# First attention: V and the transposed probabilities as high and low fp32r parts, three products in place of one fp32 product

## The chip, the cores and the metric

The kernel runs on one core of a Trainium2 chip. The time is the device time of one execution in microseconds. An engine is called by its name in the profile: PE is TensorE (PEld its weight loads), DVE is VectorE, ACT is ScalarE, POOL is GpSimd, SP is SyncE, which here only issues DMAs.

## The reference, cut to what matters

Two layers, each attention-like block plus mixture of experts, on x of 2 x 1024 x 128 in fp32. The change touches the first attention, and of this batch 0 alone:

```
q = (xn @ Wq + bq) by 8 heads of 128;  k, v = xn @ Wkv + bkv, shared by the heads
q, k += sinusoidal positions
scores = q k^T / sqrt(128), causal
probs = softmax(scores);  attn = probs @ v;  out = attn (heads side by side) @ Wo
```

Behind it come a top-1 mixture of 14 experts (gelu), a selective scan (16 states, 256 channels, a recurrence over 1024 steps) and a top-2 mixture of 8 experts.

## The kernel before, in words

**Stages.** Layer norm, transposes and router logits of both batches; keys and values of batch 0; attention of batch 0 (`attention_first`, 8 heads, from about 38 to 234 us); keys and values of batch 1; the 32 tiles of the first experts, four at a time; attention of batch 1 beside the scan of batch 0; then the second experts beside the scan of batch 1. The order on each engine is written out by hand, one instruction queue per engine, tied by semaphores. DVE, ACT and PE each have their own `head` function with the same loop over `i` from 0 to 7.

**A head** (number g) works in eight iterations i, one for each block of 128 rows of queries. Row block i sees (i + 1) x 128 keys. In iteration i:

- PE (lines 1069 to 1108) makes the scores of row block i (`scores`, in batch 0 with `three`: high and low fp32r parts of Q and K, three products), adds the causal mask (bf16), in iterations 1 and 5 makes a half of a query (`query`), and then turns row block i - 2 with 128 x 128 transposes (`turn`). In iterations 0 and 1 it turns blocks 6 and 7 of the head before. Between these stand the products of turned probabilities and V (`out_part`, line 1043) and the projection (`project`).
- DVE (lines 1598 to 1616) takes the negated row maximum of block i from PSUM (`neg_max`, L1577, up to 1024 columns), in iterations 1 and 5 moves a half of the query (`q_evac`, L1568), in iterations 3 and 7 adds a projected half to X in four instructions (`add_out`, L1595). In head 0 the steps of the first router stand behind the maxima (`routing`), two of them (L1510, L1511) behind the last one.
- ACT (lines 692 to 717) copies the turned block i - 2 out of PSUM into `PT` (`keep_turned`, L682) and then takes the exponentials of block i (`exps`, L689, with the row sum), which frees the scores' bank; it also copies outputs (`out_evac`) and the query's high part (`query_high`, L668). POOL makes the query's low part (L538).

**Banks and waits.** The turned blocks go alternately to PSUM banks 4 and 5. Row blocks 0 to 3 are one part each (128 to 512 columns); blocks 4 to 7 are two, the first always 512 columns, the second 128, 256, 384 and 512. These twelve parts are counted by c from 0 to 11. Before PE writes part c, it waits until ACT has copied part c - 2 of the same bank (`s_ed`, line 1024). The products of columns 0 to 511 of the queries (group 0, four of them: 512, 384, 256, 128 columns) wait for part 3; those of the other half (group 1, eight: five of 512, then 384, 256, 128) wait for part 10 and, from their fifth on, for part 11. `out_part(g, b, 0, 0)` and `(…, 1)` stand in iterations 6 and 7, `(…, 2)` and `(…, 3)` in iteration 0 of the next head, group 1 in its iterations 2 to 5.

**Last head.** `head_end` does what is left: turn 6, two products, turn 7, the eight products of group 1, two projections with a DVE update after each. PE goes on with batch 1 only after the last update (`s_we`), and SP starts the third group of expert weights only then.

**Memory.** `ROOM` is one array that the stages share. KB is 256 elements of a partition. `PT` lies at 29 to 53 KB, `V` at 10 to 14 KB. The first two groups of expert weights and rows, loaded during the attention, lie at 53 to 73 KB and 74 to 82 KB, the fourth group's rows at 90 to 92 KB.

## Time and profile before

| | us |
|---|---|
| median of 3 runs | 770.08 (768.84 to 777.02) |
| profiled execution, its time | 773.8 |
| its span, first to last instruction | 772.0 |
| PE busy in the span | 677.2 (88%) |
| DVE busy | 536.7 (70%) |
| ACT busy | 410.4 (53%) |
| POOL busy | 235.4 (30%) |
| PE matmuls of probabilities and V (L1043), both attentions | 141.7 in 384 records |

PE matmuls are pipelined, so the durations of neighbours overlap: what a matmul costs in a stream is the distance from its start to the next one's, not its own duration. One fp32 matmul with a V block as weights shows as two records. In a timeline a row may stand for several equal instructions in a row (x4), with the time from the first one's start to the last one's end. In brackets stands the idle time of the engine before it, and what it waited for.

### The profile page before, as it was taken

To read this page: it belongs to the slowest core of one execution; us is meant where nothing else is said; L and a number is where in the kernel's file an instruction comes from. 1 tells how busy PE (TensorE), PEld (TensorE's weight loads), DVE (VectorE), ACT (ScalarE), POOL (GpSimd) and SP (SyncE) were. 2 spreads that over 40 slices of the span, in tenths; PEclk is the share of its full clock that TensorE was granted. 3 is DMA by queue.
4 is the path that set the end of the run, shared out by engine and by line. 5 is a ranking of instruction groups with operands and counts; after the bars stand their busy time and mean duration, and the time that the engine had idled before them with its cause. 6 is when DMAs were issued, how large, how long until landed. Compare 5 with 4: busy or idle time off the path is not lost. (4 is left out here: it accounts for less than half of the span.)

```text
span 772.0 us, 11210 instructions
## 1 busy us (share of the span) xinstructions
PE 677.2 (88%) x3446; PEld 470.6 (61%) x3446; DVE 536.7 (70%) x830; ACT 410.4 (53%) x824; POOL 235.4 (30%) x183
## 2 busy tenths in 40 slices
PE   3988999999998989888899999998577889889575
PEld 2856777777766975444465566565532788888223
DVE  6165444444422225219899999999899799999998
ACT  1145665565641547375876676665543767576220
POOL 0012211221200007000023323324014846688874
PEclk9999999999996899899999999999759999999698
DMA  8400000000055671002267777868683445454112
GB/s 300 145 4 11 11 5 7 14 10 8 11 165 177 187 244 48 8 7 98 73 164 170 178 186 194 185 171 219 177 208 75 132 137 172 138 178 127 31 42 81
DMA packets 59806, 86.79 MB, mean 112 GB/s; under 512 B 7505, under 2 KB 35922, under 8 KB 59762
## 3 DMA queue, kind: packets, MB, share of 16 engines
q1 hardware_dynamic: 41330, 57.89, 24.1%
q0 software_dynamic: 7680, 23.08, 14.0%
q10 hardware_dynamic: 10752, 5.24, 2.3%
q8 instruction: 26, 0.43, 0.2%
q14 instruction: 18, 0.15, 0.1%
HBM read 54.60 MB, written 14.81 MB: 90 GB/s over the span
## 5 line engine op out<-in xcount | busy, mean ns | idle before, releaser
L1577 DVE TENSOR_REDUCE nmax<-PS 128x1 f32<-128x128 f32 (+7 forms) x128 | 96.1, 751 | 108.7 <-PE PS L1015 108.4
L1043 PE MATMUL PS<-ROOM 128*128 128x512 f32 (+3 forms) x384 | 141.7, 489 | 0.7 <-ACT ROOM L682 0.7
L682 ACT COPY ROOM<-PS 128x512 f32<-128x512 f32 (+1 forms) x192 | 85.9, 483 | 91.5 <-PE PS L1027 90.6
L689 ACT ACTIVATE ROOM<-PS,nmax 128x128 f32<-128x128 f32 (+7 forms) x128 | 95.7, 748 | 47.5 <-DVE nmax L1577 45.2
L559 POOL DMA_DIRECT2D ROOM<-ROOM x32 | 28.5, 890 | 212.7 <-DVE ROOM L1661 212.7
L1027 PE MATMUL PS<-CST,ROOM 128*128 128x128 f32 x576 | 85.1, 275 | 7.9 <-ACT ROOM L682 7.9
L1027 PEld LDWEIGHTS PS<-CST,ROOM 128*128 128x128 f32 x576 | 63.8, 141 | 35.1 <-issue 24.4
L1043 PEld LDWEIGHTS PS<-ROOM 128*128 128x128 f32 x384 | 65.0, 191 | 29.8 <-issue 25.8
L1012 PE MATMUL PS<-LATER 128*128 128x512 f32 (+2 forms) x192 | 73.5, 492 | 6.5 <-ACT ROOM L689 3.9
L1653 DVE TENSOR_TENSOR_SCAN ROOM<-ROOM 128x1024 f32<-128x1024 f32 x32 | 72.8, 2275 | 0.8 <-ACT ROOM L725 0.2
L538 POOL TENSOR_TENSOR QL<-ROOM,QH 128x512 fp32r<-128x512 f32 x16 | 20.3, 1269 | 169.0 <-ACT QH L668 169.0
L524 POOL DMA_INDIRECT rows_in<-XN,slot x48 | 65.6, 1367 | 20.0 <-issue 12.4
L530 POOL DMA_INDIRECT GA<-rows_out,slot x32 | 33.8, 1055 | 89.0 <-DMA rows_out<-ROOM 79.6
L603 POOL TENSOR_TENSOR ROOM<-ROOM 128x1024 f32<-128x1024 f32 x24 | 56.3, 2367 | 11.6 <-DVE ROOM L1834 11.6
L1012 PEld LDWEIGHTS PS<-LATER 128*128 128x128 f32 x192 | 33.6, 191 | 36.2 <-issue 24.7
L1209 PE MATMUL PS<-ROOM,LATER 128*128 128x128 f32 x384 | 53.4, 286 | 1.9 <-ACT ROOM L798 1.7
L1209 PEld LDWEIGHTS PS<-ROOM,LATER 128*128 128x128 f32 x384 | 50.7, 201 | 5.8 <-ACT ROOM L798 2.3
L1223 PE MATMUL PS<-ROOM,LATER 128*128 x384 | 50.9, 285 | 0.3
L998 PE MATMUL PS<-KH,QH 128*128 128x512 f32 (+2 forms) x96 | 46.9, 488 | 4.7 <-POOL QL L538 2.8
L1223 PEld LDWEIGHTS PS<-ROOM,LATER 128*128 128x128 f32 x384 | 47.6, 199 | 2.3 <-issue 1.9
L870 ACT ACTIVATE ROOM<-ROOM,a_sc 128x1024 f32<-128x1024 f32 x32 | 36.4, 1143 | 19.8 <-DVE ROOM L1821 17.1
L1595 DVE SCALAR_TENSOR_TENSOR X<-PS,rinv,X 128x128 f32<-128x128 f32 x128 | 35.7, 341 | 14.6 <-PE PS L1065 14.6
(178 smaller groups left out, 1248.3 us busy)
## 6 DMA issues: line engine op xcount, KB each, us to landing
ROOM<-bc_rows SPq DMA_DIRECT2D x32, 512.0 KB, 4.1
ROOM<-ROOM POOLq DMA_DIRECT2D x32, 512.0 KB, 6.0
LATER<-in_w SPq DMA_DIRECT2D x48, 256.0 KB, 2.9
ROOM<-in_w SPq DMA_DIRECT2D x32, 321.0 KB, 4.0
rows_in<-zero SPq DMA_DIRECT2D x20, 256.0 KB, 3.2
LATER<-rows_in SPq DMA_DIRECT2D x24, 128.0 KB, 2.5
rows_out<-ROOM ACTq DMA_DIRECT2D x24, 128.0 KB, 2.0
ROOM<-rows_in SPq DMA_DIRECT2D x8, 256.0 KB, 4.3
```

Of the source, the lines that this page charges most:

```text
L524: nc.gpsimd.indirect_dma_start(out=xs[m > 0][:, :], out_offset=bass.IndirectOffsetOnAxis(ap=slot[m][:, k, u:u + 1], axis=0), in_=XN[:, t, ...
L603: nc.gpsimd.tensor_tensor(YA1[:, c, :], YA1[:, c, :], HC[:, c, :], ALU.add).then_inc(s_ya, 1)
L682: nc.scalar.copy(dst, src).then_inc(s_ed, 1)
L689: nc.scalar.activation(PR[:, s, 0:nk], sc[:, 0:nk], ACT.Exp, bias=nmax[:, i % 4:i % 4 + 1], accum_out=rsum[:, i:i + 1]).then_inc(s_ex, 1)
L998: mm(dst, a[0][ra], b_[0][rb], start=first, stop=False, skip_group_check=True)
L1012: mm(dst, Q1[:, i * P:(i + 1) * P], K1[:, lo:hi], start=True, stop=False, skip_group_check=True)
L1027: r = nc.tensor.transpose(PS[:, 4 + c % 2, (j - lo) * P:(j - lo + 1) * P], PR[:, i % 2, j * P:(j + 1) * P], ident)
L1043: r = mm(PS[:, 6, lo:BANK], V[:, j, :], PT[:, 4 * group + j, lo:BANK], start=j == 0, stop=True, skip_group_check=True)
L1209: r = mm(PS[:, 5 + i, c * P:(c + 1) * P], mw1[:, 2 * s + i, c * P:(c + 1) * P], MXT1[:, 2 * s + i, :], start=True, stop=True)
L1223: r = mm(PS[:, 7, i * P:(i + 1) * P], MH1[:, 4 * i + c, :], second_w[:, bass.ds(e, 1), c * P:(c + 1) * P].rearrange("p o m -> p (o m)"), s ...
L1577: nc.vector.tensor_reduce(nmax[:, i % 4:i % 4 + 1], sc[:, 0:(i + 1) * P], AX_X, ALU.max, negate=True).then_inc(s_nm, 1)
L1653: nc.vector.tensor_tensor_scan(HS0, DA[:, c, :], drive, 0.0, ALU.mult, ALU.add).then_inc(s_xsn, 1)
```

## The change

In batch 0, V is kept as VH and VL and the turned probabilities as PTH and PTL, all fp32r. ACT's copies write the high parts (VH, PTH; the type of the destination rounds them). DVE subtracts the high part from the value that still is in PSUM and writes the low part. Each product of probabilities and V becomes three: high x high, high x low, low x high (`three`, as in the scores). PE's waits for a turned part in batch 0, for its bank and for its product, go to the new semaphore `s_el`, which DVE raises after its subtraction. In DVE's loop `turned_low` stands last in each iteration, behind `add_out`. Batch 1 stays as it is.

```diff
@@ -134,10 +134,18 @@
 
         KB = 256
         HEAD_END, MOE_END, END = 53 * KB, 90 * KB, 133 * KB
+        with ExitStack() as first_split:
+            def split_tile(name, shape, dt=F32R):
+                return first_split.enter_context(nc.sbuf_tensor(name, shape, dt))
+
+            split_tile("under_PTH", [P, 29 * KB], F32)
+            PTH = split_tile("PTH", [P, 12, BANK])
+            split_tile("under_PTL", [P, MOE_END + 2 * KB - HEAD_END], F32)
+            PTL = split_tile("PTL", [P, 12, BANK])
+            VH, VL = (split_tile(n, [P, TB, D]) for n in ("VH", "VL"))
+            split_tile("under_KH", [P, END - MOE_END - 34 * KB], F32)
+            KH, KL, QH, QL = (split_tile(n, [P, T]) for n in ("KH", "KL", "QH", "QL"))
         ROOM = sb("ROOM", [P, END])
-
-        with ExitStack() as first_split:
-            KH, KL, QH, QL = (first_split.enter_context(nc.sbuf_tensor(n, [P, T], F32R)) for n in ("KH", "KL", "QH", "QL"))
         LATER = sb("LATER", [P, 4 * T])
         K1, Q1 = LATER[:, 0:T], LATER[:, T:2 * T]
 
@@ -233,6 +241,7 @@
         s_ke = sem("keys_ready")
         s_vp = sem("values_in_psum")
         s_ve = sem("values_ready")
+        s_vl = sem("values_low_ready")
         s_ein = sem("gate_exponent_in")
         s_eout = sem("gate_exponent_out")
         s_ohb = sem("onehot_ready")
@@ -254,6 +263,7 @@
         s_ex = sem("probs_ready")
         s_tc = sem("probs_transposed")
         s_ed = sem("probsT_ready")
+        s_el = sem("probsT_low_ready")
         s_pv = sem("head_out_in_psum")
         s_ue = sem("head_out_ready")
         s_ri = sem("inverse_sum_ready")
@@ -652,7 +662,7 @@
 
                 for q in (2 * b, 2 * b + 1):
                     act.wait_ge(s_vp, q + 1)
-                    nc.scalar.copy(V[:, 4 * (q % 2):4 * (q % 2) + 4, :], bank(VALUE_BANK[q])).then_inc(s_ve, 1)
+                    nc.scalar.copy((V if b else VH)[:, 4 * (q % 2):4 * (q % 2) + 4, :], bank(VALUE_BANK[q])).then_inc(s_ve, 1)
                     if b == 0:
                         act.wait_ge(s_kf, 2 * q + 2)
                         nc.scalar.copy(KH[:, (q % 2) * BANK:(q % 2 + 1) * BANK], QF).then_inc(s_kh, 1)
@@ -673,12 +683,12 @@
                 nc.scalar.activation(Q1[:, hf * BANK:(hf + 1) * BANK], bank(7), ACT.Identity, bias=bq[:, h:h + 1]
                                      ).then_inc(s_qr, 1)
 
-            def keep_turned(g, i):
+            def keep_turned(g, i, split=False):
 
                 for part in range(1 if i < 4 else 2):
                     c = i if i < 4 else 4 + 2 * (i - 4) + part
                     act.wait_ge(s_tc, 12 * g + c + 1)
-                    dst, src = turned(PT, i, part, c)
+                    dst, src = turned(PTH if split else PT, i, part, c)
                     nc.scalar.copy(dst, src).then_inc(s_ed, 1)
 
             def exps(g, i):
@@ -705,9 +715,9 @@
                     if i == 6 and pending:
                         out_evac(1, 2 * g)
                     if i < 2 and pending:
-                        keep_turned(g - 1, 6 + i)
+                        keep_turned(g - 1, 6 + i, split)
                     if i >= 2:
-                        keep_turned(g, i - 2)
+                        keep_turned(g, i - 2, split)
                     exps(g, i)
                     if i == 1 and not split:
                         query_out(g, 1)
@@ -730,9 +740,9 @@
                 with act.Fori(1, 7) as g:
                     head(g, True, True)
                 head(7, True, False, True)
-                keep_turned(7, 6)
+                keep_turned(7, 6, True)
                 out_evac(0, 15)
-                keep_turned(7, 7)
+                keep_turned(7, 7, True)
                 out_evac(1, 16)
 
             def front():
@@ -981,7 +991,7 @@
             logits(0)
             logits(1)
             pe.wait_ge(s_ke, 2)
-            pe.wait_ge(s_ve, 2)
+            pe.wait_ge(s_vl, 2)
 
             def query(g, h, b, hf):
 
@@ -1015,13 +1025,15 @@
                 mm(PS[:, s + i // 4, (i % 4) * P:(i % 4 + 1) * P], identb[:], causalb[:], start=False, stop=True,
                    skip_group_check=True).then_inc(s_qk, 1)
 
-            def turn(g, i, first=False):
+            def turn(g, b, i, first=False):
+
+                left = s_ed if b else s_el
 
                 pe.wait_ge(s_ex, 8 * g + i + 1)
                 for part in range(1 if i < 4 else 2):
                     c = i if i < 4 else 4 + 2 * (i - 4) + part
                     if not (first and c < 2):
-                        pe.wait_ge(s_ed, 12 * g + c - 1)
+                        pe.wait_ge(left, 12 * g + c - 1)
                     lo, hi = 4 * part, min(i + 1, 4 * part + 4)
                     for j in range(lo, hi):
                         r = nc.tensor.transpose(PS[:, 4 + c % 2, (j - lo) * P:(j - lo + 1) * P],
@@ -1030,18 +1042,23 @@
 
             def out_part(g, b, group, part, free=True):
 
+                ready = s_ed if b else s_el
                 if part == 0:
-                    pe.wait_ge(s_ed, 12 * g + (11 if group else 4))
+                    pe.wait_ge(ready, 12 * g + (11 if group else 4))
                     if group or not (isinstance(g, int) and g == 0):
                         pe.wait_ge(s_ue, 2 * g + group)
                     if not (group or free):
                         pe.wait_ge(s_rkr, b + 1)
                 if part == 2 and group:
-                    pe.wait_ge(s_ed, 12 * g + 12)
+                    pe.wait_ge(ready, 12 * g + 12)
                 for j in ((2 * part, 2 * part + 1) if group else (part,)):
                     lo = max(0, j - 4 * group) * P
-                    r = mm(PS[:, 6, lo:BANK], V[:, j, :], PT[:, 4 * group + j, lo:BANK], start=j == 0, stop=True,
-                           skip_group_check=True)
+                    if b:
+                        r = mm(PS[:, 6, lo:BANK], V[:, j, :], PT[:, 4 * group + j, lo:BANK], start=j == 0, stop=True,
+                               skip_group_check=True)
+                    else:
+                        r = three(PS[:, 6, lo:BANK], (VH, VL), (PTH, PTL), (slice(None), j, slice(None)),
+                                  (slice(None), 4 * group + j, slice(lo, BANK)), j == 0)
                 if part == 3:
                     r.then_inc(s_pv, 1)
 
@@ -1090,9 +1107,9 @@
                         parity[0] = 1 - s
                         query(g + 1, h + 1, b, 0)
                     if i < 2 and pending:
-                        turn(g - 1, 6 + i)
+                        turn(g - 1, b, 6 + i)
                     if i >= 2:
-                        turn(g, i - 2, isinstance(g, int) and g == 0)
+                        turn(g, b, i - 2, isinstance(g, int) and g == 0)
                     if i == 0 and pending:
                         out_part(g - 1, b, 0, 2)
                         out_part(g - 1, b, 0, 3)
@@ -1108,10 +1125,10 @@
                         out_part(g, b, 0, i - 6, not opening)
 
             def head_end(g, b, h):
-                turn(g, 6)
+                turn(g, b, 6)
                 out_part(g, b, 0, 2)
                 out_part(g, b, 0, 3)
-                turn(g, 7)
+                turn(g, b, 7)
                 for part in range(4):
                     out_part(g, b, 1, part)
                 pe.wait_ge(*((s_qr, 2 * g + 3) if g == HEADS else (s_we, 2 * g)))
@@ -1558,6 +1575,10 @@
                     ts(QF, QF, SCALE, None, ALU.mult).then_inc(s_kf, 1)
                     dve.wait_ge(s_kh, q + 1)
                     tt(KL[:, sl], QF, KH[:, sl].bitcast(F32), ALU.subtract).then_inc(s_ke, 1)
+                    dve.wait_ge(s_ve, q + 1)
+                    t4 = slice(4 * q, 4 * q + 4)
+                    tt(VL[:, t4, :], bank(VALUE_BANK[q]).rearrange("p (t d) -> p t d", d=D), VH[:, t4, :].bitcast(F32),
+                       ALU.subtract).then_inc(s_vl, 1)
 
             keys_values(0)
 
@@ -1576,6 +1597,14 @@
                 sc = PS[:, 2 * s:2 * s + 2, :].rearrange("p a n -> p (a n)")
                 nc.vector.tensor_reduce(nmax[:, i % 4:i % 4 + 1], sc[:, 0:(i + 1) * P], AX_X, ALU.max,
                                         negate=True).then_inc(s_nm, 1)
+
+            def turned_low(g, i):
+
+                for part in range(1 if i < 4 else 2):
+                    c = i if i < 4 else 4 + 2 * (i - 4) + part
+                    dve.wait_ge(s_ed, 12 * g + c + 1)
+                    dst, src = turned(PTL, i, part, c)
+                    tt(dst, src, turned(PTH, i, part, c)[0].bitcast(F32), ALU.subtract).then_inc(s_el, 1)
 
             def inverse(g, s, earlier=True):
                 dve.wait_ge(s_ex, 8 * g + 4 + 4 * s)
@@ -1612,6 +1641,10 @@
                         q_evac(g + 1, 0)
                     if i == 7 and pending:
                         add_out(g - 1, 1, x_prev)
+                    if i < 2 and pending and not batch[0]:
+                        turned_low(g - 1, 6 + i)
+                    if i >= 2 and not batch[0]:
+                        turned_low(g, i - 2)
                     for step in after.get(i, ()):
                         step()
 
@@ -1620,6 +1653,9 @@
                         6: lambda: tile_experts(m), 7: lambda: pick_weights(m)}
 
             def head_end(g):
+                if not batch[0]:
+                    turned_low(g, 6)
+                    turned_low(g, 7)
                 inverse(g, 1)
                 add_out(g, 0, True)
                 add_out(g, 1, True)
```

## Rows read from the trace of the kernel before

**Rows 1.** Stretch of heads 1 to 7: from:to, length, each engine's busy time, granted clock, DMA.

```profile
75.00:220.00 145.00, 144.31 (x797) 104.62 (x796) 61.20 (x123) 83.76 (x203) 28.82 (x26) 1.00 0.07 21
```

**Rows 2.** PE in order of time: start, us, what; heads 1, 6 and 7.

```profile
61.45 0.94 PE L1027 MATMUL PS<-CST,ROOM 128*128 128x128 f32 x7
...
67.17 0.28 PE L1027 MATMUL PS<-CST,ROOM 128*128 128x128 f32 x1
...
197.84 0.23 PE L1015 MATMUL PS<-causalb,identb 128*128 128x128 bf16 x1
...
199.57 0.94 PE L1027 MATMUL PS<-CST,ROOM 128*128 128x128 f32 x7
...
202.33 1.04 PE L1027 MATMUL PS<-CST,ROOM 128*128 128x128 f32 x8
...
203.81 0.28 PE L1027 MATMUL PS<-CST,ROOM 128*128 128x128 f32 x1
...
205.64 1.05 PE L1065 MATMUL PS<-ROOM 128*128 128x128 f32 x8
...
207.00 0.40 PE L1000 MATMUL PS<-KH,QL 128*128 128x512 f32 x1
207.23 0.23 PE L1015 MATMUL PS<-causalb,identb 128*128 128x128 bf16 x1
...
210.00 0.27 PE L999 MATMUL PS<-KL,QH 128*128 128x128 f32 x1
210.11 0.27 PE L1000 MATMUL PS<-KH,QL 128*128 128x128 f32 x1
...
212.95 0.28 PE L999 MATMUL PS<-KL,QH 128*128 128x256 f32 x1
213.07 0.28 PE L1000 MATMUL PS<-KH,QL 128*128 128x256 f32 x1
```

**Rows 3.** DVE in order of time: 512-column operations, keys' stage and first experts.

```profile
33.58 0.75 DVE L1552 SCALAR_TENSOR_TENSOR ROOM<-PS,bk,ROOM 128x512 f32<-128x512 f32 x1
34.36 0.43 DVE L1558 TENSOR_SCALAR ROOM<-ROOM 128x512 f32<-128x512 f32 x1
35.47 0.69 DVE L1560 TENSOR_TENSOR KL<-ROOM,KH 128x512 fp32r<-128x512 f32 x1 [0.68 <-ACT KH L658]
...
255.91 0.69 DVE L1710 TENSOR_TENSOR ROOM<-PS,ROOM 128x512 f32<-128x512 f32 x1 [1.87 <-PE PS L1169]
```

**Rows 4.** DVE in order of time, end of head 6 and of head 7.

```profile
198.11 1.22 DVE L1577 TENSOR_REDUCE nmax<-PS 128x1 f32<-128x1024 f32 x1 [3.04 <-PE PS L1015]
199.25 1.12 DVE L1595 SCALAR_TENSOR_TENSOR X<-PS,rinv,X 128x128 f32<-128x128 f32 x4
200.28 0.28 DVE L1577 TENSOR_REDUCE nmax<-PS 128x1 f32<-128x128 f32 x1
...
219.61 1.22 DVE L1577 TENSOR_REDUCE nmax<-PS 128x1 f32<-128x1024 f32 x1 [2.66 <-PE PS L1015]
```

**Rows 5.** ACT in order of time: copy of row block 7's first half, head 7.

```profile
202.97 0.59 ACT L682 COPY ROOM<-PS 128x512 f32<-128x512 f32 x1 [0.71 <-PE PS L1027]
```

**Rows 6.** Head 0: a stretch, and DVE in order of time at its end.

```profile
52.00:64.00 12.00, 9.97 (x57) 7.45 (x56) 11.32 (x25) 6.83 (x14) 1.27 (x1) 1.00 0.00 0
...
61.75 1.22 DVE L1577 TENSOR_REDUCE nmax<-PS 128x1 f32<-128x1024 f32 x1
...
63.58 0.29 DVE L1577 TENSOR_REDUCE nmax<-PS 128x1 f32<-128x128 f32 x1
```

**Rows 7.** PE in order of time: the eight last products of head 7.

```profile
223.99 5.86 PE L1043 MATMUL PS<-ROOM 128*128 128x512 f32 x16 [0.24 <-ACT ROOM L682]
```

**Rows 8.** PE in order of time: the router logits ahead of the first query.

```profile
30.91 6.85 PE L948 MATMUL PS<-wgate,XNT 128*128 128x14 f32 x32
```

**Rows 9.** A stretch, and PE in order of time, between head 7 and batch 1's keys.

```profile
230.00:235.00 5.00, 2.56 (x16) 2.02 (x15) 2.25 (x8) 0.47 (x1) 0.00 (x0) 0.93 0.00 0
...
234.33 3.66 PE L966 MATMUL PS<-XNT,ROOM 128*128 128x512 f32 x4 [1.22 <-DVE X L1595]
```

## The prediction

> **What bounds the kernel now.** I started from the stretches (the view that sums each engine's busy time). In 145 us of heads 1 to 7 of the first attention, PE is busy 144.31 us at full granted clock, DVE 61.20 and ACT 83.76 [rows 1]. The reader should see that nothing but PE's stream of work sets the pace there, and that DVE looks as if it had room. Then PE's timeline, for the period: the one-block transpose of row block 0 starts at 67.17 in head 1 and at 203.81 in head 7 [rows 2], so a head takes 136.64 / 6 = 22.77 us. Last the order of work on DVE and ACT around one head's end, because the change puts twelve instructions into DVE's queue and lets PE wait for them.
>
> **What it removes.** Twelve products of probabilities and V per head (six 512 wide, two each of 384, 256 and 128), each two records. One transpose (0.11) and four records of 512 go from 203.81 to 205.64, so a record is 0.43 and a 512-wide product 0.86 us; by columns 384 is 0.64, 256 is 0.43, 128 is 0.215. Sum 6 x 0.86 + 2 x (0.64 + 0.43 + 0.215) = 7.73 us.
>
> **What it adds on PE.** Three fp32r products each. The kernel has such products already, in the scores: start to start 0.23 at 512, 0.12 at 256, 0.11 at 128 [rows 2]; between these 384 is 0.18 (an estimate). Three times (6 x 0.23 + 2 x (0.18 + 0.12 + 0.11)) = 6.60 us. So PE is spared 1.13 us a head: 0.17 for each product of 512, 0.10 for 384, 0.07 for 256, and 0.12 lost for each of 128. By iteration of the head that is -0.34 in 2 and in 3, -0.27 in 4, +0.05 in 5, -0.17 in 6, -0.10 in 7, +0.05 in 0. The narrow rows show that three products do not cost three quarters of an fp32 one at every width. The Trainium skill (FP8 and Floating Point Precision, "TensorE Precision Notes") says that true fp32 makes four passes through the array, while reduced precision reads fp32 and truncates it. By that rule, with one pass per reduced product, the saving would be a quarter of 7.73, 1.93 us; the 128-wide row, as dear as the 256-wide, speaks against it.
>
> **What it adds on DVE.** Twelve subtractions per head, from PSUM and SBUF into fp32r. No row has exactly this. The nearest are 0.69 for 512 columns: from PSUM and SBUF into f32, and from SBUF alone into fp32r [rows 3]. Ends: 0.43, the multiply by a constant in SBUF, and 0.75, bias and position added from PSUM, both for 512 [rows 3]. I take 0.69, and by the maxima's 128 columns at 0.28 [rows 4] I put 0.42 at 256 and 0.55 at 384. The next DVE instruction starts about 0.08 before the one ahead ends: the 1.22 us maximum is followed after 1.14 [rows 4]. All twelve cost about 6.7 us, which DVE has. But it works in order, and PSUM bank and product now wait for the subtraction, not for ACT's copy. Two places have no room.
>
> **Stretch A, end of iteration 7 to the transposes of row block 6.** These need the bank whose first half of row block 5 must be subtracted. In DVE's queue that subtraction stands behind the 1024-column maximum of iteration 7 and four updates of X. Now: last score product 197.84, DVE's maximum 198.11, updates 199.25, done at 200.28 [rows 2, 4]. The subtraction then takes 0.69, and an engine starts some 0.06 after the one it waits for (200.28 + 0.69 + 0.06 = 201.03). PE started these transposes at 199.57. From 197.84 that is 3.19 instead of 1.73: **+1.46**; the 0.10 spared in iteration 7 is inside it, lost.
>
> **Stretch B, from there to the transposes of row block 0.** They need the first half of row block 7. PE reaches that turn 2.76 us later (199.57 to 202.33), plus 0.05 for the narrow products. ACT begins its copy 0.64 later (202.97) and takes 0.59 [rows 5]; then 0.05, 0.69, 0.06. Sum 4.84 instead of 4.24 (199.57 to 203.81): **+0.60**.
>
> **Rest of the head.** Iterations 2 to 6 keep their lead (a maximum, a copy and a subtraction fit between the turns of one bank), and PE gains 0.34 + 0.34 + 0.27 - 0.05 + 0.17 = 1.07. A head thus takes 1.46 + 0.60 - 1.07 = **0.99 us longer**. From head 1 to head 7: six times, 5.9 us.
>
> **Head 0.** Routing shares DVE, busy 11.32 of 12 us [rows 6]. Subtractions of row blocks 1 to 4 (less 0.08 each: 0.34 less what little idle there is, 0.27; 0.48; 0.61; 0.61 and 0.20) come ahead of the last maximum, which moves from 61.75 to about 63.9. From this maximum to the next, 61.75 to 63.58, are 1.83 us; then 0.69 and 0.06: the transposes of block 6 start at 66.5 instead of 61.45, and with B's 4.84 those of head 1's block 0 at 71.4 instead of 67.17 [rows 2]: +4.2. The cover that hid ACT's copies in head 0 is gone.
>
> **Tail.** In head 7 iterations 2 to 6 give back 1.07. From the last maximum (219.61) the group of eight products began 4.38 later, at 223.99 [rows 4, 7]. Now there are 1.14 + 1.03 + 0.69 + 0.06 = 2.92 to the turn of block 6, then twice copy and subtraction with nothing between, 2 x 2.03: 6.98, +2.6. The eight products are 5 x 0.17 + 0.10 + 0.07 - 0.12 = 0.9 shorter. Tail +1.7.
>
> **Costs nothing.** The low parts of V, two times 0.69 on DVE, fall under the 6.85 us of router logits that start at 30.91 and end at 37.8 [rows 8]: the key's last subtraction starts at 35.47, 0.6 later with one before it, and the last of V ends at 37.5. If the logits were shorter, 1.4 us would show. ACT writes its copy in another type, same size. The new tiles lie in the room of later stages; the first two groups of expert weights do not touch them. All that follows waits for attention's end, so the delay is passed on whole.
>
> **Clock.** PE stood half idle from 230 to 235, and its next four records of 512 took 3.66 us instead of 1.72 [rows 9]: half speed, 1.2 GHz for a few us. In head 0 PE now waits three times for DVE, each time behind a routing step: for block 3's subtraction (the second part of block 4's turn needs its bank), for block 4's near 63.8, just ahead of the last maximum, and for block 5's until 66.5. So I add one such loss, 1.9 us, in head 1. The Trainium skill (TensorE: Matmul & The Clock Gate, "What's actually happening") has the half rate as the default that activity lifts; these rows agree.
>
> **Sum.** 4.2 + 5.9 - 1.07 + 1.7 + 1.9 = 12.6 us on the profiled execution's 773.8. That stands 0.5% above the median 770.08, which I scale from: **782.7**.
>
> **Rivals.**
> 1. *PE stays the bound, both waits covered.* Then only PE's sum counts: 8 x 1.13 = 9.0 us less, **761.1**, faster. For it: DVE is under half busy. Against: stretch A has 1.6 us of PE work over a chain of 3.2; it decides only if the maximum, the updates and the subtraction together fall under half of what the rows say. 0.06.
> 2. *Each fp32r product costs a quarter of the fp32 one at every width*, as it nearly does at 512 (0.23 of 0.86). Then a head is spared a quarter of 7.73, 1.93 instead of 1.13: 0.80 more, 6.4 in all, **776.3**, within 1%. Against it the 128-wide rows. 0.09. (The page of the Trainium skill on floating point, named above, would have it so.)
> 3. *The subtraction costs 0.43.* A and B fall by 0.26 each, a head is +0.47, head 0 +2.9, tail +0.9: 5.5 us without a clock loss, **775.6**. 0.09.
> 4. *The waits of 1.6 and 0.6 us let the clock fall in every head.* Six more times 1.9: **794**. For it: the wait before 234.33 was only 1.22. Against: from 52 to 64 PE is idle for 2 of 12 us and keeps full clock [rows 6]. 0.09.
>
> The forecast keeps 0.67. With 0.75 for a subtraction and the clock lost twice it gives 787; with small errors in the handovers 789. Range 775.5 to 789: it takes in rivals 2 and 3. Within 1% (762.4 to 777.8) is what a measurement can't tell from no change: rivals 2 and 3 less some, plus a little of the forecast's own spread, 0.17. Slower 0.77, faster 0.06.
>
> **What would show it.** PE waits for DVE's subtraction ahead of block 6's turn, about 1.5 us, and of block 0's, about 0.5, in each head; head period 23.8; the subtraction 0.69 at 512; head 1's block 0 turned near 71; DVE near 16 us of each head. It is wrong if the period is below 22.8, if PE has no idle time named for DVE, or if later stages take in the delay.

## The result and the profile after

The changed kernel took 783.38 us in the median of 20 runs (776.23 to 791.28), against 771.08 us of 20 runs of the kernel before. The ratio of the compared runs is 1.0139, with a 95% interval of 1.0106 to 1.0171: slower by 1.1 to 1.7%, or some 8 to 13 us. The ratio leaves out the three runs that stand more than 1.5% above the fastest of their kernel (788.31 and 791.28 after, 777.02 before). The prediction was 782.7.

One profiled execution is worse evidence than these medians, since the clock's phases differ from run to run. The one of after took 777.78 us with a span of 775.9, only 3.9 more than before. Cut in three: up to the first query it was 2.5 us quicker (first query at 35.09, before 37.60). The **stage** from that query to the first key product of batch 1 took 243.26 - 35.09 = 208.17 us, before 234.33 - 37.60 = 196.73: +11.4. What follows was 5.0 us shorter (775.9 - 243.26 against 772.0 - 234.33), where the change has nothing to do and the clock was kinder: granted clock 0.94 in the first 56 us of that part instead of 0.85 (that this accounts for all 5.0 us is not shown). So I compare stages below; whole times stand beside them with their ratios.

The stretch of heads 1 to 7, as in [rows 1] (columns as there):

```profile
75.00:220.00 145.00, 133.46 (x825) 110.07 (x824) 93.73 (x195) 82.04 (x196) 28.90 (x26) 1.00 0.03 9
```

PE's busy time fell from 144.31 to 133.46 us at full clock, and DVE's rose from 61.20 to 93.73. Neither is full now: the stretch has 11.5 us in which PE waits. The view of waits for 75 to 215 us (who waited for whom: us in total, times, longest) says for whom; before, PE had no wait in it:

```profile
DVE nmax L1598 <- PE PS L1025: 38.8, 29, 2.3
PE PS L1039 <- DVE PTL L1607: 11.0, 12, 1.5
```

L1607 is the subtraction, L1039 the transposes (L1027 before). Twelve waits in six heads, two each. PE in order of time in head 1, at the end of head 6 and in head 7, to be held against [rows 2], and the last group, against [rows 7]:

```profile
68.47 0.30 PE L1039 MATMUL PS<-CST,ROOM 128*128 128x128 f32 x1 [0.46 <-DVE PTL L1607]
...
187.94 0.30 PE L1039 MATMUL PS<-CST,ROOM 128*128 128x128 f32 x1 [0.45 <-DVE PTL L1607]
...
203.70 0.23 PE L1025 MATMUL PS<-causalb,identb 128*128 128x128 bf16 x1
...
206.97 0.95 PE L1039 MATMUL PS<-CST,ROOM 128*128 128x128 f32 x7 [1.50 <-DVE PTL L1607]
...
211.89 0.30 PE L1039 MATMUL PS<-CST,ROOM 128*128 128x128 f32 x1 [0.45 <-DVE PTL L1607]
...
233.81 0.50 PE L1008 MATMUL PS<-PTH,VH 128*128 128x512 f32 x1 [0.96 <-DVE PTL L1607]
```

The head period is (211.89 - 68.47) / 6 = 23.90 us, before 22.77. DVE at the same place, to be held against [rows 4]:

```profile
203.97 1.22 DVE L1598 TENSOR_REDUCE nmax<-PS 128x1 f32<-128x1024 f32 x1 [1.99 <-PE PS L1025]
205.11 1.12 DVE L1624 SCALAR_TENSOR_TENSOR X<-PS,rinv,X 128x128 f32<-128x128 f32 x4
206.15 1.01 DVE L1607 TENSOR_TENSOR PTL<-PS,PTH 128x512 fp32r<-128x512 f32 x2
```

The reader should see the chain: DVE waited 1.99 us for the last scores, then maximum, four updates and two subtractions run without a gap, and PE, idle for 1.50 us, starts at 206.97, about 0.13 after the first subtraction's end (206.15 + 0.69). A single subtraction of 512 columns took what the nearest rows had ([rows 3]; this one is in head 7):

```profile
221.71 0.69 DVE L1607 TENSOR_TENSOR PTL<-PS,PTH 128x512 fp32r<-128x512 f32 x1
```

### The profile page after: what moved, and what is told of

It reads as the page before. It is cut to its first block and busy times, and to the rows that moved or that the text cites. A ratio compares the mean times of both kernels' runs of the same rounds, so it can differ in the third digit from the quotient of the medians.

```text
span 775.9 us, 11548 instructions
## 1 busy us (share of the span) xinstructions
PE 658.3 (85%) x3530; PEld 476.0 (61%) x3542; DVE 582.5 (75%) x928; ACT 412.3 (53%) x824; POOL 235.2 (30%) x183
## 5 line engine op out<-in xcount | busy, mean ns | idle before, releaser
L1039 PE MATMUL PS<-CST,ROOM 128*128 128x128 f32 x576 | 86.0, 276 | 25.1 <-DVE PTL L1607 18.5
L1039 PEld LDWEIGHTS PS<-CST,ROOM 128*128 128x128 f32 x576 | 63.9, 141 | 53.8 <-issue 25.3
L692 ACT CAST PTH<-PS 128x512 fp32r<-128x512 f32 (+2 forms) x96 | 43.2, 483 | 75.2 <-PE PS L1039 75.2
L1057 PE MATMUL PS<-ROOM 128*128 128x512 f32 (+1 forms) x192 | 70.9, 490 | 0.5 <-ACT ROOM L692 0.5
L1607 DVE TENSOR_TENSOR PTL<-PS,PTH 128x512 fp32r<-128x512 f32 (+2 forms) x96 | 50.3, 551 | 10.1 <-ACT PTH L692 9.4
L692 ACT COPY ROOM<-PS 128x512 f32<-128x512 f32 (+2 forms) x96 | 43.0, 485 | 25.9 <-PE PS L1039 25.1
L1226 PEld LDWEIGHTS PS<-ROOM,LATER 128*128 128x128 f32 x384 | 49.8, 198 | 5.8 <-ACT ROOM L808 2.4
L1240 PEld LDWEIGHTS PS<-ROOM,LATER 128*128 128x128 f32 x384 | 46.2, 194 | 2.4 <-issue 2.1
L1624 DVE SCALAR_TENSOR_TENSOR X<-PS,rinv,X 128x128 f32<-128x128 f32 x128 | 35.8, 342 | 11.4 <-PE PS L1082 11.4
```

The lines of the kernel that those rows point to most:

```text
L692: nc.scalar.copy(dst, src).then_inc(s_ed, 1)
L1039: r = nc.tensor.transpose(PS[:, 4 + c % 2, (j - lo) * P:(j - lo + 1) * P], PR[:, i % 2, j * P:(j + 1) * P], ident)
L1057: r = mm(PS[:, 6, lo:BANK], V[:, j, :], PT[:, 4 * group + j, lo:BANK], start=j == 0, stop=True, skip_group_check=True)
L1226: r = mm(PS[:, 5 + i, c * P:(c + 1) * P], mw1[:, 2 * s + i, c * P:(c + 1) * P], MXT1[:, 2 * s + i, :], start=True, stop=True)
L1240: r = mm(PS[:, 7, i * P:(i + 1) * P], MH1[:, 4 * i + c, :], second_w[:, bass.ds(e, 1), c * P:(c + 1) * P].rearrange("p o m -> p (o m)"), s ...
L1607: tt(dst, src, turned(PTH, i, part, c)[0].bitcast(F32), ALU.subtract).then_inc(s_el, 1)
```

## The experiments

The theory: the three products spare PE 1.13 us a head, and two waits for DVE's subtractions (stretch A before row block 6's turn, stretch B before block 0's) cost more. The rivals: the products are not cheaper; DVE's total load sets the pace; the clock. For each kernel stand the stage, the head period (from the one-block turn, the transpose of row block 0, of head 1 to that of head 7, divided by six), and the time from the first query to head 1's one-block turn ("head 0"). All three are read from one trace of each kernel. How far such a figure scatters can be seen in head 0: after and order have the same code there and stand 0.68 us apart, since PE came to full speed about 1 us later in order, counted from the first query; so differences under 0.7 us in head 0 say nothing. The period repeats to 0.03 where no edit touches it (after 23.90, head0 23.91, dup3 23.93).

| kernel | head 0 | period | stage | ratio to before, 95% interval |
|---|---|---|---|---|
| before | 29.57 | 22.77 | 196.73 | |
| after | 33.38 | 23.90 | 208.17 | 1.0139 (1.0106 to 1.0171) |
| p_only | 29.42 | 21.60 | 187.53 | 0.9833 (0.9765 to 0.9901) |
| w_only | 32.68 | 24.99 | 216.17 | 1.0224 (1.0158 to 1.029) |
| dup6 | 34.53 | 25.09 | 217.95 | one run |
| dup3 | 34.44 | 23.93 | 209.44 | one run |
| order | 34.06 | 22.91 | 201.83 | one run |
| cover | 33.63 | 22.65 | 202.23 | one run |
| head0 | 31.82 | 23.91 | 206.71 | one run |
| all3 | 31.38 | 21.73 | 191.10 | 0.9939 (0.9913 to 0.9965) |
| all5 | 32.88 | 21.75 | 191.30 | 0.9922 (0.9899 to 0.9945) |
| before_tail | 29.40 | 22.77 | 195.66 | 0.9999 (0.9979 to 1.0019) |
| all6 | 28.94 | 21.77 | 187.53 | 0.9843 (0.9804 to 0.9883) |

### p_only: the products alone

```diff
-                        r = three(PS[:, 6, lo:BANK], (VH, VL), (PTH, PTL), ...
+                        r = three(PS[:, 6, lo:BANK], (VH, VL), (PTH, PTH), ...
-                left = s_ed if b else s_el
+                left = s_ed
```

and no `turned_low` on DVE; `ready` likewise. The kernel leaves out the low part of the probabilities, so its result is not the attention's; PE's work is that of the changed kernel.

> Left out of the computation: the low part of the probabilities. The third product takes the high part again, DVE makes no such low part, and PE waits for ACT's copy as in the kernel before. PE's work is that of the changed kernel. Theory (PE is spared 1.13 us a head, the waits for DVE eat it): the head period falls from 22.77 to 21.64 us, PE has no waits in heads 2 to 7, and the stage from the first query to batch 1's keys takes 196.73 - 9.0 = 187.7 us; whole kernel about 9 us faster than before. Rival (the three products themselves cost more than rows of the scores say, by switching between fp32 and fp32r): period 22.8 or more, no gain.

Period 21.60 (expected 21.64), stage 187.53 (187.7), 9.2 under before. The stretch of 75 to 210 us:

```profile
75.00:210.00 135.00, 134.39 (x855) 112.12 (x855) 60.31 (x122) 83.60 (x203) 28.78 (x26) 1.00 0.06 18
```

PE is the bound again, with less work per head. The saving is shown, and the products' rival is out.

### w_only: the waits alone

```diff
-                    dst, src = turned(PTH if split else PT, i, part, c)
+                    dst, src = turned(PT, i, part, c)
-                    if b:
+                    if True:
                         r = mm(PS[:, 6, lo:BANK], V[:, j, :], PT[:, 4 * group + j, lo:BANK], ...
-                    tt(dst, src, turned(PTH, i, part, c)[0].bitcast(F32), ...
+                    tt(dst, src, turned(PT, i, part, c)[0], ...
```

(and V instead of VH, for the copy and the subtraction of V, likewise).

> PE's products stay single fp32 ones from the fp32 copies; DVE makes the low parts all the same (nobody reads them) and PE waits for DVE's subtraction instead of ACT's copy. Theory: stretch A takes 3.27 instead of 1.73 us and stretch B 4.87 instead of 4.24, so the head period is 22.77 + 1.54 + 0.63 = 24.94 us; head 0 as in the changed kernel +3.8, tail +2.8: the stage takes about 196.73 + 3.8 + 13.0 + 2.8 = 216.3 us, whole kernel about 19 to 20 us slower than before. Rival (the longer stage comes from the new products, DVE's load is covered): period 22.8, no change.

Period 24.99 (expected 24.94), stage 216.17 (216.3). PE in head 7:

```profile
215.37 0.95 PE L1039 MATMUL PS<-CST,ROOM 128*128 128x128 f32 x7 [1.38 <-DVE PTL L1607]
...
220.25 0.30 PE L1039 MATMUL PS<-CST,ROOM 128*128 128x128 f32 x1 [0.46 <-DVE PTL L1607]
```

The two waits stand at the same places without the new products. Alone they cost 2.22 us a head (24.99 - 22.77); with the products they cost 23.90 - 21.60 = 2.30.

### dup6 and dup3: the same instruction at two places of the queue

```diff
+            spare = room(126 * KB, [4, P])
...
+                    if c == 6:
+                        tt(spare, src, turned(PTH, i, part, c)[0].bitcast(F32), ALU.subtract)
                     tt(dst, src, ...).then_inc(s_el, 1)
```

(`c == 3` in dup3).

> The changed kernel, with the subtraction of row block 5's first half (512 columns) done twice, the first time into a spare place. Theory (this one stands in the chain from the maximum of iteration 7 to PE's turn of block 6): all of its 0.61 us shows in each head; period 23.90 + 0.61 = 24.5 us, stage 208.2 + 8 x 0.61 = 213.0 us. Rival (DVE's total load sets the pace, or a fixed overhead of waiting): also +0.61; told apart by dup3.

> The changed kernel, with the subtraction of row block 3 (512 columns) done twice, the first time into a spare place. The same instruction as in dup6, at another place of the queue. Theory: in iteration 5 DVE has 0.7 us of idle time behind it, so the period stays within 0.1 us of 23.90; only head 0, where routing fills DVE, may grow by up to 0.6. Rival (DVE's total load sets the pace): +0.6 us per head, as in dup6.

dup3: period 23.93, nothing of 0.61 us on a head, so DVE's total load is not the pace. Head 0 grew by 1.06, more than the 0.6 expected: the wait for block 3's subtraction by 0.56 (4.07 instead of 3.51), and behind it PE still ran at half speed when it turned block 5 (six transposes in 1.36 us, in the changed kernel 0.82). dup6: four of its six head periods are 24.41 to 24.64, which is the 0.61 expected; two are 26.15 and 26.24, which was not, and the stage is 217.95 where 213.0 was expected. In these two the clock fell; the second one (the granted clock is the third number from the end):

```profile
215.00:217.00 2.00, 0.89 (x8) 0.92 (x9) 1.57 (x5) 0.23 (x1) 0.00 (x0) 1.00 0.00 0
217.00:219.00 2.00, 2.00 (x12) 1.91 (x11) 1.21 (x3) 1.65 (x5) 0.00 (x0) 0.55 0.04 8
```

PE had waited 2.01 and 2.10 us just before. In the other four heads it waited 2.00 to 2.09 us and kept full speed, and so it did behind the waits of 1.40 to 1.50 us in heads 1 to 6 of the changed kernel. So the fourth rival of the prediction names something real, at 1.7 us per fall, but in heads 1 to 7 it did not strike the changed kernel, and the length of the wait alone does not say when it does (more of this in the last section).

### order, cover: two ways out of the waits

order, on DVE:

```diff
-                    if i == 7 and pending:
+                    if i == 7 and pending and batch[0]:
                         add_out(g - 1, 1, x_prev)
...
                     if i >= 2 and not batch[0]:
                         turned_low(g, i - 2)
+                    if i == 7 and pending and not batch[0]:
+                        add_out(g - 1, 1, x_prev)
```

> The changed kernel, with DVE's subtractions in iteration 7 put ahead of the four updates of X. Theory: the 1.03 us of the updates leave the chain of stretch A, whose wait of 1.50 us falls to 0.5; the updates' result is needed only by the query of the next iteration, 2 us later. Period 23.90 - 1.0 = 22.9 us, stage 208.2 - 7 x 1.0 = 201.2 us. Rival (PE waits then for the updates at the query, or for ACT's copy): the period falls by less than 0.5.

cover, on PE in batch 0:

```diff
+                    if i == 0 and pending and not b:
+                        out_part(g - 1, b, 0, 2)
+                        out_part(g - 1, b, 0, 3)
+                    if i == 2 and pending and not b:
+                        pe.wait_ge(s_qr, 2 * g + 2)
+                        project(g - 1, h - 1, 0)
                     if i < 2 and pending:
                         turn(g - 1, b, 6 + i)
```

(and these steps left out at their old places).

> The changed kernel, DVE untouched; on PE, in batch 0, the last two products of columns 0 to 511 go ahead of the turn of row block 6, and the first projection ahead of the turn of row block 0. Theory: work that waits for nothing fills the waits: 0.7 of stretch A's 1.50, all 0.45 of stretch B's; period 23.90 - 1.15 = 22.75 us. Rival (moving work ahead only moves the wait to the next step, since block 6's copy and subtraction start no earlier): period falls by less than 0.5.

order: period 22.91, expected 22.9. cover: 22.65, expected 22.75. The four updates are 1.0 of stretch A, and both waits are waits of order, not of throughput: in order both are still there, at 0.36 to 0.46 us, in cover B's is gone and A's is 0.7 to 0.8. cover's stage, 202.23, holds a tail partly at half speed (granted clock 0.50 from 225 to 230 us), which order's, 201.83, has not.

### head0, all3, all5: where head 0 did not follow

```diff
                     neg_max(g, i)
+                    early = beside and not batch[0] and i >= 2
+                    if early:
+                        turned_low(g, i - 2)
                     if beside and i in beside:
                         beside[i]()
...
-                    if i >= 2 and not batch[0]:
+                    if i >= 2 and not batch[0] and not early:
                         turned_low(g, i - 2)
...
+                steps = routing(0)
+                late_steps = {2: (steps.pop(6),), 4: (steps.pop(7),)}
```

> The changed kernel; in head 0 the subtractions go ahead of the routing steps of their iteration, and the last two routing steps move to iterations 2 and 4 of head 1. Theory: PE's waits of 3.51 and 1.17 us in head 0 come from subtractions that stood behind routing steps; both are under 0.5 then, and head 1's one-block turn comes 4 us earlier against the first query; the period of later heads stays 23.90. Stage about 204.5 us. Rival (DVE is full in head 0, order changes nothing): under 1 us.

> All three reorderings in one kernel. Theory: the waits of stretch A (1.50, less 1.0 and 0.7) and B are gone, the period is PE's own work, 21.7 us, head 0 costs nothing against the kernel before; the tail still pays copy and subtraction twice, about +1.8. Stage 196.73 - 7 x 1.07 + 1.8 - 1 = about 190 us, so 6 to 7 us faster than before, 17 faster than the changed kernel. Rival (ACT's copy or the maxima become the bound): period 22.3 or more and no gain over before.

head0 gained 1.6 of the 4 us expected. The wait of 3.51 for block 3 was 0.58, but one of 2.51 for block 4 came up, and behind it the clock fell. In all3 the three edits add up in the heads (period 21.73, PE's own work) and the kernel is faster than before, ratio 0.9939. Its stage is 191.10, expected 190.

I read the 2.51 as a matter of order again: ACT's copy of block 4 stood behind its cast of the query, and this behind `q_evac`, which DVE did after `row_slots`. all5 moved `q_evac` ahead of `row_slots` in head 0, and changed the tail of `head_end` in batch 0 (on DVE first, then on PE):

```diff
+                    if early and i == 5:
+                        q_evac(g + 1, 0)
                     if beside and i in beside:
                         beside[i]()
...
+                out_part(g, b, 0, 2)
+                out_part(g, b, 0, 3)
                 turn(g, b, 6)
-                out_part(g, b, 0, 2)
-                out_part(g, b, 0, 3)
                 turn(g, b, 7)
+                pe.wait_ge(s_we, 2 * g)
+                project(g, h, 0)
                 for part in range(4):
                     out_part(g, b, 1, part)
-                pe.wait_ge(...)
-                project(g, h, 0)
```

> The three reorderings, and two more. In head 0, DVE moves the next query's half ahead of the row-slot steps (it stood behind them, ACT's cast of that half waited for it, and behind the cast the copy of block 4: a wait of 2.51 us on PE). In the tail PE does the last two products of columns 0 to 511 ahead of block 6's turn, and the first projection ahead of the group of eight products. Theory: head 0's wait falls from 2.51 to about 0.5, the tail loses 0.7 of its wait for block 6, fills its 0.96 us wait for block 7 with the projection and has one exchange with DVE less at its end (about 2.5 us in all): stage 191.10 - 2 - 2.5 = 186.6 us, about 10 us under the kernel before, 4 under all3. Rival (the chain of maximum, exponentials and copy sets head 0 whatever the order): stage 189 us.

> The kernel before with the tail's reordering alone, so that all5 is read rightly: it says how much of all5's gain is owed to the order of the tail, not to three products in place of one. Theory: the last exchange between PE and DVE (1.22 us of waiting and 0.86 of projection) leaves the path, the projection itself costs 0.6 ahead of the eight products: stage 196.73 - 1.1 = 195.6 us; whole kernel 1 us faster, which is hardly measurable. Rival (the tail's order is worth as much without the subtractions as with them): stage 194.2 us.

The expectation failed: head 0 took 32.88 instead of 31.38, with the wait at 3.21 (L1620 is the subtraction in all5 and all6, L1613 in all3, L1607 in head0). The same transposes, of block 5, in head0, all3 and all5:

```profile
61.54 1.51 PE L1039 MATMUL PS<-CST,ROOM 128*128 128x128 f32 x6 [2.51 <-DVE PTL L1607]
...
62.19 0.84 PE L1039 MATMUL PS<-CST,ROOM 128*128 128x128 f32 x6 [2.51 <-DVE PTL L1613]
...
59.88 1.51 PE L1039 MATMUL PS<-CST,ROOM 128*128 128x128 f32 x6 [3.21 <-DVE PTL L1620]
```

ACT had copied block 4 by 56.1 (0.74 from 55.35), but DVE reached its subtraction only at 59.05, after routing steps and a maximum without a gap. One of these routing steps took 1.37 us, where it takes 0.40 in all3, because (as the last section reads the rows) the edit had brought a POOL instruction beside it. So the transposes began 24.58 us after the first query, in all3 24.55: the edit of head 0 moved nothing. The 1.5 us were lost behind it, and by the clock: from these transposes to those of block 6 all5 took 3.72 us (59.88 to 63.60), at a granted clock of 0.50 from 60 to 62 us,

```profile
60.00:62.00 2.00, 2.00 (x9) 2.00 (x10) 1.44 (x2) 1.27 (x5) 0.00 (x0) 0.50 0.00 0
```

and all3, at full speed, 2.26 for the same work (62.19 to 64.45). In head0 the clock fell after the same wait of 2.51 that left all3 at full speed. So the longer head 0 of all5 does not show that its order is worse; it shows no gain.

The tail gained 1.4 us (one-block turn of head 7 to the keys 27.95, all3 29.34). before_tail shows that this order gives the kernel before 1.1 us in the stage and nothing measurable in the whole (0.9999, where 1.1 us would be 0.9986, inside the interval). So up to 1.1 us of what all5 and all6 gain in the stage is owed to the tail's order and not to the change.

### all6: routing out of head 0

```diff
-                late_steps = {2: (steps.pop(6),), 4: (steps.pop(7),)}
+                late_steps = {2: (steps.pop(5),), 4: (steps.pop(7),), 6: (steps.pop(6),)}
```

and `q_evac` back at its place; the tail as in all5.

> As all5, but head 0 is freed of routing: the row-slot steps go to iteration 2 of head 1, the choice of weights to 4, the experts of the tiles to 6, where DVE has idle time; the query's half stays where it was. Theory: head 0 was set by DVE's total of maxima, subtractions and routing steps, which no order inside head 0 helps (all5: 3.21 us of waiting for block 4); with 5.5 us of routing gone PE's waits in head 0 are under 1 us in sum and the clock does not fall there: first query to head 1's one-block turn 30.0 us (32.88 in all5, 29.57 before), stage 191.30 - 2.9 = 188.4 us, 8 us under the kernel before. Rival (routing steps in head 1 push its maxima behind): head 1 takes over 1 us longer than 21.7.

Head 0 took 28.94, where 30.0 was expected and 29.57 was the time before; head 1 took 21.96. PE's one wait for a subtraction in head 0 is left, 0.74:

```profile
54.55 0.33 PE L1039 MATMUL PS<-CST,ROOM 128*128 128x128 f32 x1 [0.74 <-DVE PTL L1620]
```

The stretch of 75 to 200 us, in heads 1 to 7:

```profile
75.00:200.00 125.00, 124.35 (x786) 103.35 (x785) 89.74 (x190) 77.81 (x186) 28.95 (x26) 1.00 0.03 10
```

PE is full again with DVE at 72%. Against all3, whose clock did not fall in head 0 either, head 0 gained 2.4 us. The stage is 187.53 (expected 188.4), 9.2 under before, and the kernel 1.2 to 2.0% faster than the one before: 758.57 us against 770.81. The stage accounts for 9.2 of these 12 us; the rest is within the interval. It is the version to keep.

## Why the prediction was right, step by step

- **PE's saving**, 1.13 us a head: p_only 22.77 - 21.60 = 1.17. Right, and so was reading the three products' price from the scores' rows: a quarter of the fp32 price at every width would have given 1.93. The Trainium skill (FP8 and Floating Point Precision, "TensorE Precision Notes") counts four passes for true fp32; a quarter of the price, read from that count, does not hold at 128 columns, where an fp32r product starts 0.11 us after the one before (0.12 at 256) and an fp32 one takes 0.215.
- **The subtraction** was put at 0.69 and was 0.69.
- **Stretch A**, predicted 3.19: 206.97 - 203.70 = 3.27. **Stretch B**, 4.84: 211.89 - 206.97 = 4.92. Both 0.08 over; in A, 0.07 of it is that PE started about 0.13 after DVE's end and not 0.06.
- **The rest of the head**, predicted -1.07: 203.70 - 187.94 = 15.76, before 16.82 (197.84 less 181.02, the one-block turn of head 6): -1.06.
- **Period** 23.90 where 22.77 + 0.99 = 23.76 was forecast; six of them 6.8 instead of 5.9 us.
- **Head 0**, +4.2: it was +3.8 (head 1's one-block turn 33.38 us after the first query, forecast 71.4 - 37.6 = 33.8), 0.48 of it by the clock (below), so the term was 0.9 too large. Two of the waits named are there, 3.51 for block 3 and 1.17 for block 5; for block 4 PE did not wait. From the last maximum to block 6's turn it was 2.67 (forecast 2.58); the maximum itself moved less than forecast. A routing step on 448 columns ahead of it took 1.57 us before and 0.97 after, 0.60 of the 0.9; the last section has why.
- **Tail** with head 7, -1.07 + 1.7 = +0.63: from the one-block turn to the keys 31.37 instead of 30.52, +0.85; from the last maximum to the group of eight 7.15 (226.66 to 233.81), forecast 6.98.
- **Clock**, +1.9 in head 1: wrong in place and size, and the step of the prediction that failed. It fell in head 0, in the windows below, ahead of a place where PE waits for DVE anyway (1.17 us at 63.55); only 0.48 us of it reached DVE, which waited that long for the last scores (60.88). Head 1 ran at full clock. The price was read wrong too: 3.66 us in [rows 9] runs from the first record's start to the last one's end, and was held against four distances of 0.43; the same row at full clock says 1.98 (after, at 243.26), so half speed cost 1.7 there, as in dup6.

The windows of 56 to 60 us of the changed kernel:

```profile
56.00:58.00 2.00, 1.09 (x3) 0.94 (x4) 2.00 (x4) 1.49 (x4) 1.02 (x1) 0.67 0.00 0
58.00:60.00 2.00, 2.00 (x6) 1.58 (x5) 1.93 (x4) 0.98 (x2) 0.26 (x1) 0.50 0.00 0
```

PE had been idle for 3.51 us, until 56.91, and the clock falls in the first window; DVE is busy nearly throughout both.

The sum of the stage without the clock was 10.7, and 11.4 was measured. The prediction of 12.6 for the whole lies near the difference of the medians (12.3) partly by luck: the 1.9 us of clock, of which 0.48 was there, stand against 0.9 too little in the period and 0.2 in the tail, and 0.9 too much in head 0; the ratio says 10.7. That the delay is passed on whole can't be read from the two profiled executions (what follows the stage was 5.0 us shorter); the medians and the ratio, 12.3 and 10.7 beside the stage's 11.4, bear it out. That the V parts cost nothing held: the last was done at 34.66, and the first query came at 35.09, right behind the logits as before.

The faster rival (PE stays the bound) needed both waits covered. They were not in the order as written, but all3 and all6 show that they can be: PE has no wait for DVE there in heads 2 to 6. The prediction's condition for it, that the chain itself be half as long, was too narrow: moving work ahead of the wait does it as well.

## What to carry to other kernels

Before moving work to the engine that is idle half the time, write down its queue around each place where another engine will wait for the new instruction: a busy share of 42% hid nothing here, because the subtraction stood behind a 1.2 us maximum and four updates that nobody was waiting for yet. Let the waited-for instruction go first in its queue, and put work that depends on nothing ahead of the wait on the other side; the same change then turned from 1.4% slower to 1.6% faster. Where an engine is full for a while (head 0), order helped only in part (head0: 1.6 of 4 us, all5: nothing more); taking work out did the rest (all6). And before a difference of 1 or 2 us between two traces is laid to an edit, look whether the clock was the same in both: in head 0 all5 looked 1.5 us worse than all3 by its clock alone.

## What the runs showed of the hardware that was not expected

- PE's clock stood two waits of about 1.5 and 0.45 us in each head of 23.9 us, and fell in two of six heads once the longer wait was 2.0 to 2.1 us (dup6), at 1.6 to 1.7 us of extra head time. The wait's length does not decide it: in head 0 it fell after 2.51 us in head0 and not in all3, and after 3.51 in the changed kernel and not after 3.47 in w_only (its fp32r products of 512 columns start 0.23 us apart behind the wait, 60.61 to 60.84, where they are 0.43 apart in the changed kernel). What else decides it no run here shows.
- The granted clock of the profile is not to be trusted in the first 50 us of some traces: before's reads 1.00 from 42 to 50 us, where its fp32r products of 512 columns start 0.43 us apart (49.09, 49.52). The distance between starts is the surer sign there.
- A DVE step with two SBUF inputs was held while POOL ran an elementwise step. In all5 one routing step on 224 columns took 1.37 us beside POOL's subtraction of the query (55.52 to 56.84), the like of it a moment later 0.39:

```profile
55.72 1.37 DVE L1515 TENSOR_TENSOR rt<-rt,re 128x224 f32<-128x224 f32 x1
57.12 0.39 DVE L1517 TENSOR_TENSOR rt<-rt,oh 128x224 f32<-128x224 f32 x1
...
55.52 1.32 POOL L548 TENSOR_TENSOR QL<-ROOM,QH 128x512 fp32r<-128x512 f32 x1 [7.84 <-ACT QH L678]
```

The Trainium skill (GPSIMD Engine Reference, "Specifications") names this contention for DVE instructions with two SBUF inputs; the trace agrees. No run changes this alone, but the traces hold the comparison: the routing step on 448 columns starts 0.18 to 0.19 us after POOL's instruction in before, before_tail and p_only and takes 1.56 to 1.57 us; it starts 0.78 to 0.79 us after it in after, order, cover, w_only and dup6 and takes 0.97 to 0.98; in dup3 it starts behind the other's end and takes 0.61. Whenever the two met, it ended 0.47 to 0.49 us after POOL's. The new subtractions, with one input in PSUM, kept their time beside POOL: two of them took 0.89 us in all3 (61.35, POOL from 60.91 to 62.18) and 0.88 with POOL idle in all5 (59.05).
